# A two-layer graph kernel: transposing weight loads issued in parts over a tile's slots, and the last output tile by halves

## The reference

```
h = relu(layernorm(x))                       # x: 2500 x 1024
support = h @ W0                             # 1024 x 1024
x = x + segment_sum(support[src] * edge_w[:, None], dst)     # 80000 edges
h = relu(layernorm(x))
deg = 1 + number of edges from each row
norm = deg[row] ** -0.5 * deg[col] ** -0.5
x = x + segment_sum(norm[:, None] * (h @ W1.T + b)[col], row)   # edges and a self loop on every node
```

## Time and profile before

| | |
|---|---|
| median of three runs | 1671.95 us |
| profiled execution | 1668.41 us |
| its span | 1666.6 us |
| busy TensorE matmul / DVE / ACT / POOL | 90% / 57% / 27% / 18% |
| tiles 0 to 17 of layer one (first edge matmul of tile 0 to the last slot) | 364.44 to 1038.9 us |
| layer two's matmuls | 1103.78 to 1657.9 us |

### The profile page before, as it was taken

How to read it: one execution, slowest core, us unless ns; L and a number is a source line. 1 busy time by engine, 2 the same in 40 slices (tenths; PEclk the granted TensorE clock), 3 DMA queues, 4 the chain that set the end, 5 groups by cost and what they waited for, 6 DMA issues and landing times.

```text
span 1666.6 us, 24355 instructions
## 1 busy us (share of the span) xinstructions
PE 1495.9 (90%) x7584; PEld 776.6 (47%) x7585; DVE 953.8 (57%) x1710; ACT 450.5 (27%) x883; POOL 307.3 (18%) x576
## 2 busy tenths in 40 slices
PE   3978899986998988888888988889999999999997
PEld 2444455543554444444433444334654645546455
DVE  5876655754776764545454555279745456355442
ACT  5645454521222222222222222153301103002000
POOL 2134422321232322222222222000000000000000
PEclk9989999997999999999999999989999999999999
DMA  7202411238565665556665566482330322403102
GB/s 275 102 26 67 137 25 25 49 77 169 131 156 124 142 140 132 140 126 141 141 144 132 130 141 135 127 331 70 105 119 10 131 84 81 129 15 114 60 1 74
DMA packets 411477, 185.62 MB, mean 111 GB/s; under 512 B 376875, under 2 KB 393791, under 8 KB 411342
## 3 DMA queue, kind: packets, MB, share of 16 engines
q1 hardware_dynamic: 411342, 184.03, 42.0%
HBM read 76.45 MB, written 77.11 MB: 92 GB/s over the span
## 4 chain that ended last, share of the span: by engine, by line
PE 60%; SPq 10%; DVE 9%; DMA 8%; issue 7%; ACT 3%; DVEq 1%; ACTq 1%; POOL 0%; POOLq 0%
PE pair L1752 20%; PE pair L1807 12%; PE pair L1549 10%; PE pair L1657 10%; SPq L470 6%; DMA a_scratch<-area 5%; PE pair L1561 4%; DVE area L1006 1%; DVE slots L946 1%; DVE slots L943 1%; DVE slots L947 1%; SPq L461 1%; DMA wstage<-c_scratch 1%; SPq L459 1%; SPq L493 1%
## 5 line engine op out<-in xcount | busy, mean ns | idle before, releaser
L1657 PE MATMUL pair<-h,area 128*128 128x512 f16 x2400 | 572.4, 394 | 9.1 <-issue 9.1
L1657 PEld LDWEIGHTS pair<-h,area 128*128 128x128 f16 x2400 | 240.3, 101 | 289.4 <-issue 57.1
L1752 PE MATMUL pair<-area,h 128*128 128x500 f16 x1600 | 341.6, 376 | 5.5 <-DVE h L1200 5.5
L1561 PE MATMUL pair<-slots 128*128 128x240 f16 x1124 | 152.4, 275 | 109.1 <-DVE slots L947 91.9
L1752 PEld LDWEIGHTS pair<-area,h 128*128 128x128 f16 x1600 | 156.2, 98 | 190.2 <-issue 9.9
L688 POOL TENSOR_TENSOR deg_acc<-deg_acc,area 128x320 f32<-128x320 f32 x160 | 147.0, 919 | 487.7 <-ACT area L1314 487.7
L1312 ACT ACTIVATE area<-pair 128x320 f32<-128x320 f32 x160 | 70.0, 438 | 539.7 <-PE pair L1561 393.3
L1807 PE MATMUL pair<-wmat,area 128*125 128x512 f16 x960 | 209.0, 379 | 0.0
L1006 DVE SCALAR_TENSOR_TENSOR area<-pair,area 128x320 f16<-128x320 f32 x160 | 78.0, 488 | 219.6 <-ACT area L1314 219.1
L1561 PEld LDWEIGHTS pair<-slots 128*128 128x128 f16 x1124 | 109.8, 100 | 164.6 <-DVE slots L947 111.4
L1807 PEld LDWEIGHTS pair<-wmat,area 128*125 128x125 f16 x960 | 130.7, 137 | 75.4
(11 more groups left out here) (247 smaller groups left out, 1183.3 us busy)
## 6 DMA issues: line engine op xcount, KB each, us to landing
c_scratch<-area SPq DMA_DIRECT2D x160, 160.0 KB, 2.2
a_scratch<-area SPq DMA_DIRECT2D x320, 80.0 KB, 2.2
xt<-x_scratch SPq DMA_DIRECT2D x20, 500.0 KB
out_x<-xt SPq DMA_DIRECT2D x20, 500.0 KB
xt<-in_x SPq DMA_DIRECT2D x19, 512.0 KB, 3.8
x_scratch<-xt SPq DMA_DIRECT2D x19, 512.0 KB, 2.8
wstage<-c_scratch SPq DMA_DIRECT2D x17, 500.0 KB, 5.0
slots<-c_scratch SPq DMA_DIRECT2D x17, 500.0 KB, 5.0
```

What stands on the lines that cost most here:

```text
L1561: return pe.matmul(dest, touches[:, t, 0:P], touches[:, t, P:CS], start=first, stop=last, skip_group_check=True)
L1657: last = pe.matmul(sum_pair(e)[:, half * H:(half + 1) * H], wts(e)[:, q, k, :], hpart(k, r)[:, half * H:(half + 1) * H], start=k == q == r ...
L1752: ins = pe.matmul(sums_of(c, f), hpart(k, q)[:, f * P:(f + 1) * P], counts, start=first and q == 0, stop=last and q == 1, skip_group_check ...
```

## The change

- `load_weights` takes a part j of four: the two DMAs transpose 5 of the 20 column blocks of 128 each. The buffer's semaphore becomes four, one for each part, and TensorE waits for part g/2 in slots 0, 2, 4 and 6 of the products.
- In the loop the load of tile td + 1 is issued ahead of the stores of slots 1, 2, 3 and 4 of tile td. The wait for the products of tile td - 1 and for the stores stands in part 0. The load at the end of a tile is gone. Tile 19's is issued in four parts behind the loop, tile 0's in four parts where it stood.
- The second weights are loaded in eight parts of 128 rows, two DMAs each, ahead of the store of slot 6 of tiles 3, 5, ..., 17.
- Layer two loads and stores each 125-row tile as 112 rows and 13 rows.
- Layer two's last tile does all products of columns 0 to 511, then those of columns 512 to 1023; DVE and SyncE follow by halves.

```diff
+            def load_weights(td, e, j, summed=0):
+                if j == 0:
+                    for s in range(2):
+                        sp.wait_ge(st_out[s], 3 * 16 * (QPT // 2) * (td + 1))
+                    need(sp, agg_ready, summed)
+                k0, k1 = j * T // PARTS, (j + 1) * T // PARTS
                 for q in range(2):
-                    sp.dma_start_transpose(wts(e)[:, q], a_rows[q][bass.ds(td * P, P), :]).then_inc(a_in[e], 16)
+                    sp.dma_start_transpose(wts(e)[:, q, k0:k1, :],
+                                           a_rows[q][bass.ds(td * P, P), k0 * P:k1 * P]).then_inc(a_in[e][j], 16)
...
-            load_weights(1, 1)
...
-            for q in range(2):
-                sp.dma_start_transpose(wmat[:, q], w_dram[q]).then_inc(w1_in, 16)
+            def load_w1(f):
+                for q in range(2):
+                    at = bass.ds(f * P, P)
+                    sp.dma_start_transpose(wmat[:, q, :, at], w_dram[q, at, :]).then_inc(w1_in, 16)
...
                 for q in range(QPT):
+                    if 1 <= q <= PARTS:
+                        load_weights(td + 1, 1 - e, q - 1, td)
+                    if q == QPT - 2 and e == 1 and before != 2:
+                        load_w1(i - 1)
                     store_quad(QPT * (td + PRE) + q, q % 2)
...
-                sp.wait_ge(agg_ready, td + 1)
-                load_weights(td + PRE, e)
...
             last = T // 2 - 1
+            for j in range(PARTS):
+                load_weights(T - 1, 1, j, T - PRE)
...
+            ROW_PARTS = ((0, RW // 16 * 16), (RW // 16 * 16, RW))
...
+                for a, b in ROW_PARTS:
+                    sp.dma_start(out[m * RW + a:m * RW + b, :], xt[a:b, e, :]).then_inc(y_out[e], 16)
...
+                if g % 2 == 0:
+                    pe.wait_ge(a_in[e][g // 2], 32 * (i + 1))
...
+                    halves = ((0,), (1,)) if m == T - 1 else ((0, 1),)
+                    for part, k in ((part, k) for part in halves for k in range(KD)):
```

More of the change, by code:

```diff
@@ L33, in gnn_two_layers @@
     UA, UB, QB = 2, 1, 64
+    PARTS = 4
     BT = 4
@@ L304, in gnn_two_layers @@
         st_out = [sem(f"st_out{s}") for s in range(2)]
-        a_in = [sem(f"a_in{s}") for s in range(2)]
+        a_in = [[sem(f"a_in{s}_{j}") for j in range(PARTS)] for s in range(2)]
         sel_ready = sem("sel_ready")
@@ L464, in _ @@
             a_rows = [a_dram[q].rearrange("g w (r k) n -> (g w r) (k n)", r=R) for q in range(2)]
-            def load_weights(td, e):
-                for s in range(2):
-                    sp.wait_ge(st_out[s], 3 * 16 * (QPT // 2) * (td + 1))
+            def load_weights(td, e, j, summed=0):
[4 more added lines that the diff above has]
+                k0, k1 = j * T // PARTS, (j + 1) * T // PARTS
                 for q in range(2):
-                    sp.dma_start_transpose(wts(e)[:, q], a_rows[q][bass.ds(td * P, P), :]).then_inc(a_in[e], 16)
+                    sp.dma_start_transpose(wts(e)[:, q, k0:k1, :],
+                                           a_rows[q][bass.ds(td * P, P), k0 * P:k1 * P]).then_inc(a_in[e][j], 16)
             for w in range(PQ):
@@ L484, in _ @@
                     sp.wait_ge(table_ready, 2)
-                    load_weights(0, 0)
+                    for j in range(PARTS):
+                        load_weights(0, 0, j)
             sp.wait_ge(sup_out, T)
@@ L538, in _ @@
             first_layer(0, 0, before=False)
-            first_layer(0, 1)
+            first_layer(0, 1, before=2)
             with sp.Fori(1, T // 2 - 1) as i:
@@ L570, in _, with store_last @@
             sp.dma_start(bias_b, b1.rearrange("(a n) -> a n", a=1).to_broadcast([P, D])).then_inc(b_in, 16)
+            ROW_PARTS = ((0, RW // 16 * 16), (RW // 16 * 16, RW))
             def load_rows(m):
                 e = m % 2
-                need(sp, y_out[e], 16 * (m // 2))
-                sp.dma_start(xt[0:RW, e, :], x1_dram[m * RW:(m + 1) * RW, :]).then_inc(xr_in[e], 16)
+                need(sp, y_out[e], 32 * (m // 2))
+                for a, b in ROW_PARTS:
+                    sp.dma_start(xt[a:b, e, :], x1_dram[m * RW + a:m * RW + b, :]).then_inc(xr_in[e], 16)
+            def store_last():
+                m, e = T - 1, (T - 1) % 2
+                for k in range(2):
+                    sp.wait_ge(y_ready, m + k + 1)
+                    for a, b in ROW_PARTS:
+                        sp.dma_start(out[m * RW + a:m * RW + b, k * H:(k + 1) * H],
+                                     xt[a:b, e, k * H:(k + 1) * H]).then_inc(y_out[e], 16)
             def store_tile(m):
@@ L580, in store_tile @@
                 sp.wait_ge(y_ready, m + 1)
-                sp.dma_start(out[m * RW:(m + 1) * RW, :], xt[0:RW, e, :]).then_inc(y_out[e], 16)
+                for a, b in ROW_PARTS:
+                    sp.dma_start(out[m * RW + a:m * RW + b, :], xt[a:b, e, :]).then_inc(y_out[e], 16)
             sp.wait_ge(var_ready, 8)
@@ L597, in _ @@
                                 load_counts(c + 2, j)
-                    store_tile(m)
+                    if m == T - 1:
+                        store_last()
+                    else:
+                        store_tile(m)
                     if m + 2 < T:
@@ L601, in _ @@
             for s in range(2):
-                sp.wait_ge(y_out[s], 16 * (T // 2))
+                sp.wait_ge(y_out[s], 32 * (T // 2) + 32 * s)
         CONSTS = 20
@@ L1278, in finish @@
                                                          ALU.mult, ALU.add)
-                ins.then_inc(y_ready, 1)
+                    if k == 1 or m == T - 1:
+                        ins.then_inc(y_ready, 1)
             dve.wait_ge(b_in, 16)
@@ L1801, in products @@
                         pe.wait_ge(aggs2_lo, KD * c + 2)
-                    for k in range(KD):
+                    halves = ((0,), (1,)) if m == T - 1 else ((0, 1),)
+                    for part, k in ((part, k) for part in halves for k in range(KD)):
                         if b == 0 and k > 1:
@@ L1805, in products @@
                         for q, r in ((0, 0), (0, 1), (1, 0)):
-                            for half in range(2):
+                            for half in part:
                                 last = pe.matmul(out_pair(m)[0:RW, half * H:(half + 1) * H],
@@ L1810, in products @@
                                                  stop=k == KD - 1 and q == 1)
-                    last.then_inc(wout2_ready, 1)
+                        if k == KD - 1:
+                            last.then_inc(wout2_ready, 1)
                     if b == 0:
@@ L1819, in _ @@
             sums_of_first()
-            pe.wait_ge(w1_in, 32)
+            pe.wait_ge(w1_in, 32 * KD)
             products(0)
```

6 lines of the change are left out of this document (3 added, 3 removed).

## The result

The changed kernel takes 1602.47 us (median of four runs, 1600.25 to 1603.71) against 1671.16 for the kernel before on the same chip: a ratio of 0.9585, with a 95% interval of 0.9569 to 0.9602. The direction was forecast rightly, the size was not: 1560 was predicted, with 1600 as the upper end of the range. The profiled execution took 1603.71 us, of which the span is 1601.9. Its own forecast was 1556.7, so 47.0 us are to be found.

The account below looks back on a forecast made before the run. TensorE was taken to bound a slot, with stalls in slots 3 and 4 from SyncE's transposing loads holding up stores. Profiled execution: 1668.4 - 108.7 + 1.8 - 4.8 = 1556.7 us; median 1671.95 - 111.7 = 1560, range 1548 to 1600.

Parts of the forecast that it names:

- So 5 blocks cost 0.92 and 8 blocks 1.3: SyncE's issue price in us for small transposes, from a line through 20 and 64 blocks; range 0.7 to 1.6.
- They fit, barely: Tiles 6 to 17: two parts with register work take 2.05 us of the 2.13 us gap between SyncE's stores.
- SyncE does not keep pace: Rival: small transposes cost well above the line; 1585 us at 1.3 a part, about 1618 at 1.6; chance 0.27.
- up to 2 us of lateness costs nothing: Late SyncE stores are hidden by ACT's buffer slack and DVE's one-hot lead; above that each microsecond shows on TensorE.
- which leaves 0.7: ACT's buffer slack of 1.7 us shrinks to 0.7 when a store lands behind transposes, in 3.03 us instead of 2.04.
- does not touch: Stall at DVE's back edge, 2.3 to 4.6 us of TensorE six times, 18.8 us together, was taken as unaffected.
- Slots 3 and 4, minus 108.7: Stalls in slots 3 and 4 of all 18 tiles vanish without the 5.8 us block at the tile's end: minus 108.7 us.
- minus 50: Weak bound of the slots 3 and 4 gain in us, if parts cost 1.6: 4.5 a tile lost in tiles 6 to 17.
- Tile 0's load: Ahead of the loop, four parts take 7.6 us of SyncE for 5.8, covered by other work: 0 (bounds 0 to 1).
- Tile 19's load, plus 1.8: Behind the loop, eight issues take 7.6 us for 5.5, delaying layer two's counts: plus 1.8 us (0 to 3).
- The end, minus 4.8: Layer two's end: halves save 0.7 us and the split last store 4.1, together minus 4.8 (minus 1 to minus 5.5).
- SyncE's loop body: Rival: the longer body raises SyncE's back edge from 0.25 us towards 4.01, costing up to 16 us: 1576; chance 0.08.

Follow-up runs that it names:

- e7: Ten-block kernel with tile 0's weights loaded as separate transposes of 1, 2, 4, 13, 5 and 15 blocks, each alone in flight; up to 5 blocks 1.20 us an issue.
- e4: Against e0: DVE's loop over tiles 6 to 17 written out, so that it has no back edge; 1584.61 us, ratio 0.9500.
- e2: Against e0: the second weights loaded behind the loop in two transposing DMAs; 1594.10 us, ratio 0.9555.
- e3: Against e0: one transposing DMA of 10 blocks a slot instead of two of 5, same bytes in the same slots; 1575.83 us, ratio 0.9440.
- e8: Against e0: 10-block issues, second weights behind the loop, and both of DVE's loops written out; 1540.02 us, ratio 0.9215.
- e0: The changed kernel plus one register instruction per slot on ACT, the yardstick for the other runs; 1602.37 us, ratio 0.9609.
- e1: Kernel before with only layer two's part of the change: 112 and 13 rows, last tile by halves; 1661.46 us, ratio 0.9952.
- e9: Kernel before with only DVE's two loops written out; 1641.14 us, ratio 0.9836.
- e10: Kernel before with only the second weights' load moved behind the loop, unsplit; 1650.15 us, ratio 0.9885.
- e6: e8 plus tile 0's load in two parts and, behind the loop, layer two's first counts ahead of tile 19's weights; 1533.01 us, ratio 0.9187.
- e5: Against e0: 10-block issues and the second weights behind the loop, DVE's loops kept; 1562.95 us, ratio 0.9372.

## Why the prediction was wrong

**The failed step: "So 5 blocks cost 0.92 and 8 blocks 1.3", and "They fit, barely".** 5 blocks cost 1.20. With a sum that filled the gap "to 0.1 us", 0.28 us twice a slot is all it takes: SyncE's slot is 4.43 us in place of 3.57 (1.52 + 2.05), and TensorE's is 3.65. Of the 0.86 too many the two issues make 0.56; the other 0.3 is register work between the DMAs, 0.51 us a slot (4.43 - 1.52 - 2.40) where 0.2 was taken, and the price alone would have been enough. The upper bound, 1.6, held the value, and the rival "SyncE does not keep pace" named the mechanism; at 1.3 a part it gave 1585. That was too little for the lateness that builds up over four slots; measured are 1602. And 0.60 stood on the two points, whose common line says nothing of the floor below it (`e7`). Two sizes on one line do not say that a third, four times smaller, lies there too.

**The second failed step: "up to 2 us of lateness costs nothing".** The size of this cover was about right; the lateness went beyond it, and it met a place that draws on the same lead. In slots 3 and 4 TensorE loses only 0.3 us in 18 tiles, but the buffer of slot 4's store, 3.6 us late in tile 15, is wanted two slots on. ACT's copy in slot 6 starts 3.56 us behind the edge matmuls instead of the 0.61 of slots 1 to 4, so it is 2.9 late and 0.7 was covered, as forecast ("which leaves 0.7"). DVE comes to its back edge as late: it is done 2.1 us behind the start of slot 7, in the kernel before 0.8 us ahead of it. Without a back edge this lateness still costs TensorE 0.8 to 1.5 us in slot 7 of tiles 7 to 15 (`e4`). With it, no lead is left to hide the wait there. I had costed the back edge as something that the change "does not touch"; its ends went from 18.8 to 42.0 us, and the even ends from nothing to 13.8. The second weights' store in slot 6 was forecast 1 us late and is 4.0 late in tile 15, yet what they cost comes from a longer back edge (`e2`). By undoing: the parts' price 23 us of the slots' losses (`e3`), the back edge 20.5 (`e4`), the second weights 8.8 (`e2`), together 52 of the 56 that `e8` takes away.

**Slots 3 and 4, minus 108.7.** Right to 0.3 us. The bound for parts of 1.6 ("minus 50") put the lateness in the wrong place. It stands at the tile's end. The prediction also set the 4.45 us of the products after a stall against 3.24; the usual time of the same 15 matmuls is 3.40, and 3.24 is from their start to the next edge matmul.

**Tile 0's load.** "7.6 us of SyncE" is 11.23 in one block, as the timeline shows, and the store due at 334.6 goes out at 340.0. Tile 0's slot 0 loses 2.5 us, 0.5 more than before, and its first edge matmul starts 1.4 later (365.87 against 364.44). Forecast 0 to 1. That start is not a steady number: `e0`, with the same load, has 364.64, and `e1`, with the old one, 366.83. So no cost of this part is shown:

```profile
328.74 11.23 SPq L476 DMA_TRANSPOSE area<-a_scratch  x8
340.01 0.59 SPq L460 DMA_DIRECT2D c_scratch<-area  x1
```

**Tile 19's load, plus 1.8.** From the last slot (968.53) to layer two's long sums (1052.26) it is 83.7 us against 78.2: plus 5.5, of 0 to 3. The eight issues take 11.29 and not 7.6, and SyncE comes to them 2.4 us later, with the second weights ahead. The store of x does land sooner (2.91 against 4.37 in the earlier trace rows), as was guessed. Three more runs of the old order behind the loop (`e1`, `e9`, `e10`) have 76.0 to 76.4 in place of 78.2, so the cost is 5.5 to 7.7. `e8`, with 10-block issues and the second weights out of the loop, has 77.3; `e6` puts the counts first as well, and there the same way takes 980.89 - 910.7 = 70.2. SyncE's timeline and TensorE's, changed kernel:

```profile
968.54 3.05 SPq L504 DMA_TRANSPOSE wmat<-w_scratch  x2
...
977.28 11.29 SPq L476 DMA_TRANSPOSE area<-a_scratch  x8
988.61 0.58 SPq L509 DMA_DIRECT2D x_scratch<-xt  x1
```

```profile
1052.26 4.36 PE L1786 MATMUL pair<-area,h 128*128 128x500 f16 x13 [2.67 <-DVE h L1231]
```

**The end, minus 4.8.** Minus 5.2, inside its bounds; `e1` shows it by itself. The wait for the store is 1.5 us, under the 2.0 to 2.5 taken. The timeline answers to the earlier trace rows: one operation of DVE behind TensorE's last half.

```profile
1567.08 31.27 PE L1842 MATMUL pair<-wmat,area 128*125 128x512 f16 x144
...
1593.28 0.75 DVE L1307 SCALAR_TENSOR_TENSOR xt<-pair,dinv_u,xt 125x512 f32<-125x512 f32 x1 [2.58 <-PE pair L1842]
...
1598.39 0.75 DVE L1307 SCALAR_TENSOR_TENSOR xt<-pair,dinv_u,xt 125x512 f32<-125x512 f32 x1 [4.36 <-PE pair L1842]
```

**SyncE's loop body.** It did not become too long. In the changed kernel SyncE's branch back takes 0.24 to 0.28 us at each of its seven turns, as in the kernel before (0.25 to 0.28). A turn has 217 to 219 recorded instructions against 190 to 192.

**The account.** Of the 47.0 us missed, slots make 40.6 (108.7 less the 68.1 saved), tile 0's start 1.4, the way behind the loop 3.7, layer two's rest 1.7, the end -0.4. Only the first, the third and the last can be put down to the change. Tile 0's start varies by more, as said; and layer two's 1.7 stands between the start of the long sums and those of the next chunk, which lie 106.4 us apart here and 104.7 in the kernel before, but 104.7 in `e0` too and 106.3 in `e1`.

The Trainium skill ("Runtime: NRT & Kernel Launch", "Instruction fetch mechanics") was used ahead for SyncE's loop, where it held. It says as well that straight code streams while a far branch stalls on a fetch; `e9`, where DVE's code is straight and the tile ends fall from 20.7 to 2.2 us, agrees. That DVE's branch is a far one is not shown: a turn of DVE's second loop has 186 recorded instructions, fewer than SyncE's 218, and only the code that its branches skip could make its body longer.

## What to carry to other kernels

A queue that has to keep a pace is sized by its sum over a slot: when the forecast fills the slot to a tenth of a microsecond, the price of one issue decides everything, and a price from sizes where the transfer holds the issue must not be extended down. Slack between engines is one account: before "lateness up to x costs nothing" is written, follow it to where the late thing is next wanted, here two slots on, and to the next place that draws on the same slack, here a loop's back edge. Splitting a block evenly is right, but with as few and as large pieces as the gap takes: one piece of 10 blocks for 1.33 us and not two of 5 for 1.20 each.

## What the runs showed of the hardware

- Issuing a transposing DMA holds SyncE for about 1.20 us whatever its size up to 5 blocks of 128x128 (2-byte elements), for 1.33 with 10, 1.43 with 13, 1.69 with 15 (`e7`, `e3`), 2.79 with 20 and 8.26 with 64 (kernel before). One plain DMA of a quad's store takes 0.37 (changed kernel).
- The wait at DVE's back edge, 3.6 to 4.0 us in tiles 6 to 17 of the kernel before and 4.7 at the end of tile 3, is gone when the loops are written out, and with it 28 us (`e9`). SyncE's own back edge takes 0.25 us.
- DVE's back edge takes longer when transposing DMAs are issued shortly ahead of it: 3.73 to 3.85 us against 2.75 to 2.92 (`e0`, `e2`), 4.53 to 5.12 against 3.80 to 4.30 (`e3`, `e5`), at the ends of tiles 9 to 15. Why is open.
- 4.4 us of idle time of TensorE are followed by products that take 4.33 instead of 3.40 us for 15 matmuls, at a granted clock of 0.50 at first and 0.78 in the mean. The slot behind such a stall lost 1.5 to 3.0 us at the odd ends from tile 7 on (changed kernel), beside the stall itself.
